# Eight constant candidates for the radius limit, flags and branches by pairs of tiles, and searches that begin two tiles ahead, in a nearest-neighbour graph convolution

## What is computed

```python
x_flat = gn(x)                             # group norm, (B, N, C)
emb = x_flat @ dist_w.T                    # 32 wide
d2 = sq[:, :, None] + sq[:, None, :] - 2 * emb @ emb.T
adj = (24 nearest of each row) & (sqrt(d2) <= 10)  |  eye(N)
X_lin = x_flat @ fc_w.T + fc_b
Dv, De = adj.sum(axis=2), adj.sum(axis=1)
out = (adj / De) @ adj.T / Dv @ X_lin + x_flat
out = x + silu(batch_norm(out))            # statistics over all four images
```

## Time and profile before

| | us |
|---|---|
| median of three runs (191.45 to 192.35) | 191.46 |
| the profiled execution | 191.39 |
| its span | 189.4 |
| TensorE busy, weight loads apart | 160.3 |
| VectorE busy | 153.0 |
| ScalarE busy | 114.0 |
| GpSimd busy | 101.3 |

### The profile page before, as it was taken

How to read it: one execution, slowest core, us unless ns; L and a number is a source line. 1 busy time by engine, 2 the same in 40 slices (tenths; PEclk the granted TensorE clock), 3 DMA queues, 4 the chain that set the end, 5 groups by cost and what they waited for, 6 DMA issues and landing times.

```text
span 189.4 us, 4274 instructions
## 1 busy us (share of the span) xinstructions
PE 160.3 (85%) x1273; PEld 100.8 (53%) x1277; DVE 153.0 (81%) x908; ACT 114.0 (60%) x193; POOL 101.3 (53%) x140
## 2 busy tenths in 40 slices
PE   7888997998969996799999887999999979999200
PEld 2323532473628744566667544556556658789200
DVE  1566999999998639999997499976979996799773
ACT  2144868997693959925552987444319564672391
POOL 1003436669994794993222299998466956520000
PEclk9999999999978999889999999999999999999965
DMA  5801000435344860972293148384472673597047
GB/s 181 296 36 2 2 3 1 58 57 98 74 57 57 71 46 2 189 95 55 55 94 47 31 129 96 60 86 83 58 31 28 117 151 73 96 215 297 5 155 290
DMA packets 44939, 16.94 MB, mean 89 GB/s; under 512 B 41832, under 2 KB 42472, under 8 KB 44912
## 3 DMA queue, kind: packets, MB, share of 16 engines
q1 hardware_dynamic: 44048, 16.24, 46.8%
q10 hardware_dynamic: 864, 0.40, 0.8%
HBM read 6.11 MB, written 2.13 MB: 44 GB/s over the span
## 4 chain that ended last, share of the span: by engine, by line
PE 32%; POOL 25%; issue 21%; ACT 12%; DVE 6%; ACTq 1%; DVEq 0%; POOLq 0%
PE pg L402 9%; POOL H L778 8%; PE pt L427 8%; PE pt L468 4%; PE po L365 4%; POOL x_wide L753 4%; PE pt L492 4%; ACT left L573 3%; PE po L389 3%; ACT key L623 3%; POOL wide_a L753 2%; POOL xn L764 2%; ACT sign L631 2%; POOL tw L745 2%; DVE xn L1075 2%
## 5 line engine op out<-in xcount | busy, mean ns | idle before, releaser
L876 DVE MAX8 cand<-key 128x8 f32<-128x64 f32 x512 | 81.4, 212 | 0.7
L427 PEld LDWEIGHTS pt<-xp,H 128*128 128x128 bf16 x768 | 46.2, 100 | 17.7 <-issue 13.8
L623 ACT ACTIVATE key<-pg 128x512 f32<-128x512 f32 x64 | 34.7, 593 | 33.6 <-PE pg L402 33.3
L427 PE MATMUL pt<-xp,H 128*128 128x128 bf16 (+1 forms) x768 | 51.3, 225 | 0.4 <-DVEq L926 0.4
L402 PE MATMUL pg<-right,left 64*128 64x512 f32 x128 | 40.7, 648 | 5.5 <-ACT key L623 4.6
L631 ACT ACTIVATE sign<-key,thr 128x1024 bf16<-128x1024 f32 x32 | 36.7, 1148 | 3.9 <-DVE thr L902 3.3
L778 POOL TENSOR_SCALAR H<-sign 128x1024 bf16<-128x1024 bf16 x32 | 33.4, 1044 | 0.0
L773 POOL TENSOR_SCALAR low<-cs 128x1 bf16<-128x1 f32 x32 | 6.8, 213 | 44.3 <-ACT sign L631 44.3
L402 PEld LDWEIGHTS pg<-right,left 64*128 64x128 f32 x128 | 12.1, 184 | 14.6 <-ACT key L623 8.1
L891 DVE MAX8 top<-cwork 128x8 f32<-128x128 f32 x64 | 17.8, 278 | 0.1
L891 DVE MAX8 top<-cand 128x8 f32<-128x128 f32 x32 | 9.2, 288 | 5.3 <-DVE cand L876 2.7
(11 more groups left out here) (95 smaller groups left out, 229.4 us busy)
## 6 DMA issues: line engine op xcount, KB each, us to landing
x_sb<-x SPq DMA_DIRECT2D x1, 2048.0 KB, 10.3
out<-xn SPq DMA_DIRECT2D x7, 256.0 KB, 2.3
dvb<-inv_rows SPq DMA_DIRECT2D x3, 512.0 KB, 5.2
x_sb<-x SPq DMA_DIRECT2D x1, 1024.0 KB, 6.1
x_sb<-x SPq DMA_DIRECT2D x1, 512.0 KB, 3.8
HT<-H SPq DMA_TRANSPOSE x32, 3.5
x_sb<-x ACTq DMA_DIRECT2D x1, 256.0 KB, 3.2
x_sb<-x SPq DMA_DIRECT2D x1, 256.0 KB, 3.5
```

Source lines behind the costliest of these rows:

```text
L427: mm = pe.matmul(pt[:, j // T_BLOCKS, at:at + wide], lhs, x_cols(b, t, q, wide), start=(t == 0 and j % T_BLOCKS == 0 and q == 0), stop=(t ...
L623: act.activation(key[:, k % KEYS, cols], pg[:, h, :], ACT.Copy).then_inc(s["drained"], 1)
L876: ins = dve.max(cand[:, k % 2, c, :], key[:, k % KEYS, c * CHUNK:(c + 1) * CHUNK])
```

## The change

- Row 1 of `cwork` is eight elements longer, and these are set once to `LAST_IN`. The third MAX8 reads 136 elements and writes the threshold itself. L902 is gone.
- The noise bound is tested afterwards: GpSimd subtracts threshold from noise and compares with zero for two tiles at a time, and this becomes one more flag a tile. A tile whose threshold lies above the bound takes the slow selection.
- Flags go by `GROUPS`: 15 pairs of tiles and the last two tiles alone. TensorE sums four columns at once, VectorE takes their least by one reduction, and one branch serves both tiles.
- A pair is released four searches after its first tile; the table `SETTLE` has it, `FLAG_STEP` the turn of the flag on TensorE. The last tiles come sooner.
- The first two chunks of tile k+2 are issued at the end of search k, ahead of the branch; the other chunks move by two places.
- `scale_t` for images 0 and 1 comes one search later (searches 12 and 20), for image 2 where it was (26). The four `out_part` have their own table, `OUT_STEPS`.
- X of image 2 is filled in turn 13, not 8 and 9, X of image 3 in turn 21, not 18. The gathers begin one or two turns later: image 0 in turns 15 to 19, image 1 in 22 to 26, image 2 in 28 to 31. `WIDEN` follows.
- There are two places for X, not three, ten for keys, not eight, six for thresholds, not four; esq uses a part of `prod`.

```diff
+KEYS = 10
 HS = 6
 SIGNS = 3
-THRS = 4
+THRS = 6
 FLAGS = 4
-XBUFS = 3
+XBUFS = 2
 LAG = 3
 AHEAD = 4
-SCALE_STEP = {1: LAG, 2: LAG, 3: LAG - 1}
+GROUPS = [(k, k + 1) for k in range(0, ALL - 2, 2)] + [(ALL - 2,), (ALL - 1,)]
+SETTLE = [g[0] + 4 for g in GROUPS[:10]] + [23, 25, 27, 29, ALL - 2, ALL - 1, ALL]
+FLAG_STEP = [g[0] + 3 for g in GROUPS[:10]] + [22, 24, 26, 28, ALL - 2, ALL - 1, ALL]
+LAST_STEP = {1: 3, 2: 3, 3: 2}
+SCALE_STEP = {1: 4, 2: 4, 3: 2}
+OUT_STEPS = {18: (0, 0), 21: (0, 1), 27: (1, 0), 28: (1, 1)}
 EMB_STEPS = {0: 1, 5: 2, 10: 3}
-WIDEN = {6: [(0, 0)], 7: [(0, 1)], 8: [(0, 2), (0, 3)], 12: [(0, 4), (0, 5)], 14: [(0, 6), (0, 7)],
-         22: [(2, 0)], 23: [(2, 1)], 25: [(2, 2), (2, 3)], 26: [(2, 4), (2, 5)], 28: [(2, 6), (2, 7)]}
-X_STEPS = {3: [(1, 0)], 4: [(1, 1)], 8: [(2, 0)], 9: [(2, 1)], 18: [(3, 0), (3, 1)]}
+X_MIDDLE = {1: (0, 1), 4: (1, 0), 5: (1, 1), 14: (2, 0), 15: (2, 1), 23: (3, 0), 26: (3, 1)}
+X_LOW = {2: (0, 1), 5: (1, 0), 6: (1, 1), 14: (2, 0), 15: (2, 1), 23: (3, 0), 26: (3, 1)}
+WIDEN = {6: [(0, 0)], 8: [(0, 1), (0, 2)], 9: [(0, 3)], 11: [(0, 4)], 13: [(0, 5)], 16: [(0, 6), (0, 7)],
+         22: [(2, 0), (2, 1)], 24: [(2, 2), (2, 3)], 25: [(2, 4), (2, 5)], 27: [(2, 6), (2, 7)]}
+X_STEPS = {3: [(1, 0)], 4: [(1, 1)], 13: [(2, 0), (2, 1)], 21: [(3, 0), (3, 1)]}
 T_BLOCKS = HALF // (C + 1)
 T_BANKS = -(-TILES // T_BLOCKS)
...
-        GATHER = {13: (0, 6), 14: (0, 7), 15: (0, 7), 16: (0, 6), 17: (0, 6),
-                  21: (1, 10), 22: (1, 10), 23: (1, 10), 24: (1, 9), 25: (1, 9),
-                  27: (2, 7), 28: (2, 7), 29: (2, 7), 30: (2, 7), 31: (2, 4)}
-        RELEASE = {k: [k - LAG] if k >= LAG else [] for k in range(ALL)}
-        RELEASE.update({k: [k - LAG + 1] for k in range(ALL - TILES, ALL)})
-        RELEASE.update({ALL - TILES - 1: [ALL - TILES - 4, ALL - TILES - 3], ALL - 2: [ALL - 4, ALL - 3], ALL - 1: [ALL - 2],
-                        ALL: [ALL - 1]})
+        GATHER = {15: (0, 7), 16: (0, 7), 17: (0, 6), 18: (0, 6), 19: (0, 6),
+                  22: (1, 10), 23: (1, 10), 24: (1, 10), 25: (1, 9), 26: (1, 9),
+                  28: (2, 8), 29: (2, 8), 30: (2, 8), 31: (2, 8)}
...
-            def flag(k):
-                pe.wait_ge(s["lowered"], k + 1)
-                if k >= FLAGS:
-                    pe.wait_ge(s["flag_read"], k - FLAGS + 1)
-                pe.matmul(flag_at(k), low[:, k % THRS:k % THRS + 1], filler[:, 0:1], start=True,
+            def flag(g):
+                pe.wait_ge(s["lowered"], 2 * (g + 1))
+                if g >= FLAGS:
+                    pe.wait_ge(s["flag_read"], g - FLAGS + 1)
+                pe.matmul(flags_at(g), filler[:, 0:1], low[:, g % FLAGS, 0:2 * len(GROUPS[g])], start=True,
                           stop=True).then_inc(s["flagged"], 1)
...
-                    settled = RELEASE[k - 1] if k > 0 else []
-                    if b > 0 and t == SCALE_STEP[b]:
+                    settled = SETTLED[k - 1] if k > 0 else []
+                    if b > 0 and t == LAST_STEP[b]:
                         for kk in settled:
                             scatter(kk)
                     if k + AHEAD < ALL:
                         fill_key((k + AHEAD) // TILES, (k + AHEAD) % TILES)
-                    early = k >= ALL - 3
+                    early = k >= ALL - 2
                     if early:
-                        flag(k - 1)
-                    if not (b > 0 and t == SCALE_STEP[b]):
+                        for g, step in enumerate(FLAG_STEP):
+                            if step == k:
+                                flag(g)
+                    if not (b > 0 and t == LAST_STEP[b]):
                         for kk in settled:
                             scatter(kk)
+                    if not early:
+                        for g, step in enumerate(FLAG_STEP):
+                            if step == k:
+                                flag(g)
                     if k in EMB_STEPS:
                         embed(EMB_STEPS[k])
                     if k - 1 in EMB_STEPS:
                         norms(EMB_STEPS[k - 1])
                     for bb, h in X_STEPS.get(k, []):
                         fill_x(bb, h)
-                    if k > 0 and not early:
-                        flag(k - 1)
...
                 b, t = divmod(k, TILES)
-                pool.wait_ge(s["signed"], k + 1)
-                if k >= THRS:
-                    pool.wait_ge(s["flagged"], k - THRS + 1)
-                pool.tensor_scalar(low[:, k % THRS:k % THRS + 1], cs[:, b, t:t + 1], float(FULL), None, ALU.is_ge)\
-                    .then_inc(s["lowered"], 1)
+                g = [k in group for group in GROUPS].index(True)
+                if k == GROUPS[g][-1]:
+                    n = len(GROUPS[g])
+                    first = t - n + 1
+                    slot = (k - n + 1) % THRS
+                    if first == 0:
+                        pool.wait_ge(s["noise_made"], 3 * (b + 1))
+                    pool.wait_ge(s["limited"], k + 1)
+                    pool.wait_ge(s["lowered"], 2 * g)
+                    pool.tensor_tensor(apart[:, 0:n], noise[:, b, first:t + 1], thr[:, slot:slot + n, 7], ALU.subtract)\
+                        .then_inc(s["apart_made"], 1)
+                    if g >= FLAGS:
+                        pool.wait_ge(s["flagged"], g - FLAGS + 1)
+                    pool.wait_ge(s["apart_made"], g + 1)
+                    pool.tensor_scalar(low[:, g % FLAGS, 0:n], apart[:, 0:n], 0.0, None, ALU.is_ge)\
+                        .then_inc(s["lowered"], 1)
+                    pool.wait_ge(s["signed"], k + 1)
+                    pool.tensor_scalar(low[:, g % FLAGS, n:2 * n], cs[:, b, first:t + 1], float(FULL), None, ALU.is_ge)\
+                        .then_inc(s["lowered"], 1)
+                else:
+                    pool.wait_ge(s["signed"], k + 1)
...
-                b, t = divmod(k, TILES)
-                def ahead(first, end):
-                    if k + 1 < ALL:
-                        candidates(k + 1, range(first, end))
                 src = cand[:, k % 2, :, :].rearrange("p c e -> p (c e)")
-                dve.wait_ge(s["step"], chain[0])
-                for r in range(3):
+                dve.wait_ge(s["step"], cand_made[k])
+                for r in range(2):
                     found = signal(dve.max(top[:, r, :], src))
-                    ahead(4 * r, 4 * r + 2)
+                    candidates(k + 1, 4 * r + 2, 4 * r + 4)
                     dve.wait_ge(s["step"], found)
-                    if r < 2:
-                        dst = cwork[:, r, :]
-                        replaced = signal(dve.match_replace(dst, top[:, r, :], src, 2 * FIRST_OUT))
-                        ahead(4 * r + 2, 4 * r + 4)
-                        dve.wait_ge(s["step"], replaced)
-                        src = dst
-                if t == 0:
-                    dve.wait_ge(s["noise_made"], 3 * (b + 1))
-                dve.tensor_scalar(thr[:, k % THRS:k % THRS + 1], top[:, 2, 7:8], LAST_IN, noise[:, b, t:t + 1],
-                                  ALU.max, ALU.min).then_inc(s["limited"], 1)
+                    replaced = signal(dve.match_replace(cwork[:, r, 0:CHUNKS * 8], top[:, r, :], src, 2 * FIRST_OUT))
+                    candidates(k + 1, 4 * r + 4, 4 * r + 6)
+                    dve.wait_ge(s["step"], replaced)
+                    src = cwork[:, 0, 0:CHUNKS * 8] if r == 0 else cwork[:, 1, :]
+                dve.max(thr[:, k % THRS, :], src).then_inc(s["limited"], 1)
-                for kk in RELEASE[k]:
-                    read_flag(kk)
+                candidates(k + 1, 10, CHUNKS)
+                for g in RELEASE[k]:
+                    read_flags(g)
                 if k == ALL - 1:
                     out_part(B - 2, 0)
-                ahead(10, CHUNKS)
+            def read_flags(g):
+                dve.wait_ge(s["flagged"], g + 1)
+                dve.tensor_reduce(least_at(g), flags_at(g), AX.X, ALU.min).then_inc(s["flag_read"], 1)
+            def release(g):
+                dve.wait_ge(s["flag_read"], g + 1)
+                dve.wait_ge(s["clipped"], GROUPS[g][-1] + 1)
+                under = dve.value_load(least_at(g).bitcast(I32))
                 with dve.If(under < UNDER_BITS):
-                    pick(k)
+                    for k in GROUPS[g]:
+                        pick(k)
                 with dve.Else():
                     dve.nop()
-                dve.sem_inc(s["h_ready"], 1)
-                dve.sem_inc(s["key_used"], 1)
+                dve.sem_inc(s["h_ready"], len(GROUPS[g]))
+                dve.sem_inc(s["key_used"], len(GROUPS[g]))
...
+                    for g in RELEASE[k]:
+                        release(g)
+                    if b > 0 and t == LAST_STEP[b] - 1:
                         invert_dv(b - 1)
-                    if b > 1 and t == 2:
-                        out_part(b - 2, 0)
-                    if b > 1 and t == 3:
```

(3 more changed lines are left out.)

85 lines of the change are left out of this document (42 added, 43 removed).

## The result

The changed kernel takes 200.15 us, the median of three runs (197.77 to 202.44), against 191.46 before: a ratio of 1.038 with an interval of 1.022 to 1.054. Timed again on another occasion beside the kernel before, it is 200.13 (197.41 to 200.68) against 191.35, ratio 1.0545 [1.0452, 1.0638]. Forecast were 188.4 and a range of 182.5 to 193. One thing has to be known in order to read the ratios: single executions of one kernel differ (the kernel before took 188.1 to 194.97 us, at mean granted clocks of 0.973 to 0.940), and a ratio with an interval is made from the means of those executions alone that lie within 1.5% of their kernel's fastest, so it can differ by a per cent from that of the medians (here 1.045 and 1.046).

A forecast was written before the change was run, and what follows sets the result against it. TensorE was taken to set the pace from about 50 us on, VectorE close behind. Walking four stretches of the new order put the last scatter at 163.6, not 166.6, tail unchanged: -3.0 us, 191.39 to 188.4; range 182.5 to 193.

The forecast's parts named there:

- the walk: Hand simulation of the new order from row prices, engine by engine: -3.0 us, to 188.4; chance 0.42 for 186 to 190.4.
- C: Rival: TensorE gives back part of its gain through clock falls after idles; time within 0.5%, 190.5 to 192.4; chance 0.17.
- D: Rival, slower: pairs make TensorE's work lumpy with idle turns, four clock falls of 1.4 cost 5.6, 194.0; chance 0.15.
- A plain search of 3.15: VectorE: a search without flag or branch falls from 3.37 to 3.15 us, L902 gone and the next MAX8 sooner.
- A pair's flag and branch of 0.6 (0.45 to 0.9): VectorE: one pair's flag reduction and branch, behind two chunks not six, cost 0.6 us; one tile's cost 0.5 before.
- 10 us off VectorE's loop, and TensorE let go by three: VectorE saves 0.3 to 0.4 a search, some 10 us over the loop; TensorE's end moves by only 3.0.
- Fill 17 at 70.4: TensorE: fill 17 begins at 70.4 us, before at 76.75, after an idle of 2.6.
- scale_t(2) at 137.3, the last scatter at 163.6: Ends forecast for VectorE's scale_t of image 2 (142.5 before) and TensorE's last scatter (166.6 before).
- The flag of tiles 20 and 21 ready at 113.3 after a wait of 1.3, that of 22 and 23 at 127.0 after 1.1: TensorE waits for two pairs' flags; the second is paced by GpSimd's work, its window of 14.36 us plus additions.
- GpSimd's small instructions, 3.4 us: GpSimd gets one small instruction more a pair, 16 x 0.21 us, counted in the time only where it is late.
- E, the slow selection: Rival: a threshold above the noise bound sends both tiles of a pair to slow selection, 18 us a pair; chance 0.02.
- Two flags off 20.59: TensorE, last stretch: 20.59 us of work less two flags, taken as 20.1, plus waits 2.5 from 141.0, ends at 163.6.

The follow-up runs named there:

- a_fill: Changed kernel plus filler matmuls on constants where TensorE idles (turns 12, 14, 27, 29); 193.08 us, ratio 1.020 to the kernel before.
- b_fill: Kernel before plus matmuls on constants, results unused, around its idle places in turns 2, 7 and 12; 191.80 us, ratio 1.012.
- after_ctl: The changed kernel without an edit, timed again on another occasion; 200.13 us, ratio 1.0545 to the kernel before.
- b_x_pairs: Kernel before with X of image 2 in turn 13, image 0's gather two turns later, tiles 9 to 14 released two at a time; 194.54 us, ratio 1.024.
- b_pairs_last: Kernel before with the last image's releases in pairs (searches 25, 27, 29), flags single; 195.07 us, ratio 1.029.
- a_all: Changed kernel with fillers in turns 12 and 14, last-image single releases, ScalarE's widening a turn later, image 2's gather and widening as before; 191.95 us, ratio 1.0135.
- a_single: Changed kernel with groups of one tile, flags and releases as in the kernel before, other tables as changed; 199.16 us, ratio 1.049.
- after: The changed kernel, first timing, without an edit; median 200.15 us, profiled execution 202.44, ratio 1.038 to the kernel before.
- a_widen: Changed kernel with ScalarE's widening of the last image's tiles one turn later; 196.65 us, ratio 1.036 to the kernel before.
- a_last: Changed kernel with flags and releases of the last image's tiles one by one, not in pairs; 198.61 us, ratio 1.047.
- a_cover: Changed kernel with VectorE's reduction of the flags ahead of the six chunks, so eight stand before the branch's load; 198.37 us, one run.
- b_const: Kernel before with the third MAX8 reading eight constants and writing the threshold, L902 gone, noise bound left out; 189.92 us, ratio 1.001.
- before: The kernel without the change; median 191.46 us, profiled at 191.39.
- b_x: Kernel before with X of image 2 filled in turn 13 and image 0's gather in turns 15 to 19; 191.53 us, ratio 1.006.
- a_fill_last: Changed kernel with filler matmuls in turns 12 and 14, single releases in the last image, ScalarE's widening a turn later; 193.84 us, ratio 1.024.
- a_fill_widen: Changed kernel with filler matmuls in turns 12, 14, 27 and 29 and ScalarE's last-image widening one turn later; 192.77 us, ratio 1.016.

## Why the prediction was wrong

The failed step is the one put as "In the walk idles of 2.6, 2.1 and 2.0 stand; I took no fall." The idles came (3.22, 2.33 and 4.23), and the clock fell behind each. It is not the only one: a_fill, whose clock does not fall up to the last scatter, still takes 193.0 in its profiled execution, 4.6 above the forecast, so the walk's waits were too short as well. Against 188.4, the profiled execution has 14.0 us more. By stations (their ends), with a_fill as the divide:

- *Clock falls, 6.7 us.* scale_t(2) ends at 147.1, in a_fill at 140.4. 2.3 of them lie ahead of scale_t(0), with the fall near 20 us, which is no work of the change (the same program, timed again, has one near 35 us in its place, and starts scale_t(0) 1.3 us earlier). The rest is that of turns 12 and 14. C and D priced a fall at 1.4; the rows behind the first two idles are worth 0.95 + 1.90 and 0.80 + 0.78, 2.2 on the mean. The walk had even counted 1.7 for the fall that the kernel before has near 79 us as given back.
- *The walk up to scale_t(2), 3.1 us.* It said 137.3. In a_fill 2.3 of them are there at the end of scale_t(0) (71.5, forecast 69.2); 0.9 of that is a wait for a key copy ahead of the fill in turn 5, which the walk did not have. From there on it is off by 0.7 in 69. So at full clock scale_t(2) starts only 2.1 us sooner than before (138.45 against 140.53) and 0.6 sooner than in b_fill (139.09), and not five.
- *The last image, 4.0 us.* From the end of scale_t(2) to that of the last scatter I walked 26.3; it is 30.3. The wait in turn 30 was forecast at 2.0 and is 4.23; the fall behind it, 1.5, was not in the walk.
- *Behind the loop, 0.2.*

after_ctl, whose profiled execution (200.31) lies at its median, has 11.9 us more than the forecast, and the same four terms are 5.0, 3.1, 3.6 and 0.2.

Point by point. *A plain search of 3.15:* 3.13. *A pair's flag and branch of 0.6 (0.45 to 0.9):* 1.13, above the upper end, since I took the load behind two chunks to be covered as behind six. *Pairs of 6.9:* 3.13 + 4.26 = 7.4, where no flag is late. *10 us off VectorE's loop, and TensorE let go by three:* its busy time fell by 7.6, but the time between is spent in waiting for flags. *15 flags, 1.4 us:* right, and small. *Fill 17 at 70.4:* 74.53; 72.18 in a_fill. *scale_t(2) at 137.3, the last scatter at 163.6:* 147.1 and 177.5. *The flag of tiles 20 and 21 ready at 113.3 after a wait of 1.3, that of 22 and 23 at 127.0 after 1.1:* in a_fill 116.8 after 1.00 and 130.1 after 0.41. *GpSimd's small instructions, 3.4 us:* 3.6, by its busy time of 104.9 against 101.3. *E, the slow selection:* it never ran. (Its MAX8 of 1024, put at 1.2 us, would be 16 x 0.14 = 2.2 by the row that it names.) *Two flags off 20.59:* that leaves 20.4, not the 20.1 of the walk, and a sum of 188.7.

*The rivals.* D named the mechanism, lumps with idle turns between them, and b_x_pairs shows it in the kernel before. I gave it 0.15 since I counted only its clock (5.6 us) on top of a walk that gained 3. What D lacked is that the same lumps also stop the last image: 2.9 us in b_pairs_last. C had the warning in hand: the idle of 1.96 ahead of fill 17 before, with a clock of 0.74 behind it. The walk lengthens just this idle, and the sum still took no fall there; it cost 2.85 us behind the 3.22 of idle.

The sum over the parts: a_fill takes 7.0 us off after_ctl, and the last image's remedies 1.1 more by medians (a_all 191.95). What stays, 1.0135 (1.008 by the medians), may be the late start of the last image's scatters, VectorE's late release (0.67 a pair), GpSimd's further small instructions, or several of them; the runs don't divide it.

## What to carry to other kernels

Where one engine hands another small pieces and is paced by a third's copies, a piece in every turn is the cover for those copies; grouping pieces in pairs saves the flags (1.4 us here) and leaves every second turn bare. Price an idle time of TensorE at its length plus the slower work behind it, and look in the profile for places that are already at the edge. An experiment that undoes a grouping must not put in costs that the kernel before did not have, as a_single did.

## What the runs showed of the hardware

- *Which idle times the clock fell behind.* These are all idle times of TensorE of 1.65 us and more, from turn 3 to the last scatter, in the profiles of the 16 kernels. TensorE was at 2.4 GHz ahead of each, and a fall to 1.2 GHz shows in the rows next behind: 2.56 for a fill that takes 1.61 after a wait, up to 4.93 for two scatters of 2.94.

| idle us | a fall behind it | none |
|---|---|---|
| 3.84, 4.23 | after_ctl, after (turn 30) | |
| 3.22, 3.23 | after, after_ctl, a_widen, a_last, a_cover (turn 12) | |
| 3.08 | | a_cover (turn 30) |
| 2.67 | a_single | |
| 2.25 to 2.37 | after, after_ctl, a_last, a_cover, b_const | a_widen, a_single twice |
| 1.96 to 2.04 | before, b_x, a_fill_last, b_x_pairs twice | b_pairs_last twice |
| 1.84, 1.89 | a_last | b_x |
| 1.65 to 1.67 (turn 3) | after_ctl, a_fill_last, a_all, a_cover | after, a_widen, a_fill, a_fill_widen, a_last |

Shorter ones are no safeguard: in the kernel before the fill behind an idle of 0.96 took 2.29, and in b_pairs_last the one at 34.02, behind 0.30 with another 1.09 shortly ahead, took 2.36. So the length of the idle time alone does not decide it, and the same program can fall in one execution and not in another (turn 3 of after and after_ctl).

- *Matmuls on constants hold the clock.* 12 of them, 2.73 us, in place of idle time kept 72.18 to 76.7 at full clock. They are no sure gain: in the kernel before they brought nothing (b_fill).
- *A register load behind the instruction that makes its value* costs 0.67 us more behind two MAX8 of 64 elements than behind eight.
